# The start of a fused attention and expert kernel: x loaded first, a chain of norm steps split up and woven into the first tiles

## The chip, the cores and the metric

The kernel runs on one core of one Trainium2 chip, as one program. The metric is the device time of one execution in microseconds, the median of three runs. The core's engines are TensorE (PE), VectorE (DVE), ScalarE (ACT), GpSimd (POOL) and SyncE (SP), which here issues most transfers. Each engine works through its own queue in order; semaphores tie the queues together.

## The reference

x is [16, 256, 128] in fp32, 4096 tokens of 128 features. What is computed, cut to what matters here:

```python
x = x + layernorm(linear_attention(layernorm(x)))      # 16 heads of 8, q and k through elu + 1, causal
x = x + layernorm(ffn(layernorm(x)))                   # shared expert + 1 of 16 experts by a router

# linear attention, per batch and head, along the sequence:
s = s + outer(k_i, v_i);  z = z + k_i
out_i = (q_i @ s) / (q_i . z + 1e-6)                   # then @ Wo + bo
```

A layernorm here has no gain and no bias: (x - mean) / sqrt(var + 1e-5).

## The kernel before

The tokens are cut into 32 tiles of 128 (NT = 32), a tile to the 128 partitions, two tiles to a sequence. The kernel has three stages. Stage 1 (`step1`) walks over the 32 tiles and does norm, projection, causal sums and output projection. Stage 2 (`step2`) walks over 8 groups of four tiles and does the shared expert and the routing. Stage 3 (`step3`) walks over 47 tiles of rows sorted by expert. Nothing is planned at run time: each engine has its own copy of the loops, and the order written there is the order of its queue.

**Ahead of stage 1.** SyncE issues the attention weights `w_qkvo`, then x in three loads of 4, 12 and 16 tiles (LOADS), into the first 128 columns of the wide tile `rows` (260 columns a row: x, the attention's result, and four more), then the FFN's weights; then, once GpSimd has zeroed 15 tiles of `rows` (line 476, 3900 elements a partition), four transfers clear the table of sorted rows, and the expert weights follow. VectorE takes the statistics of each tile (line 708) and turns them into the reciprocal deviation `rs1` and the shift `nm1` by `rstd_steps` (lines 93 to 122), 15 small steps that depend on each other: the reciprocal root is a guess by bits and two rounds of Newton's method. It does so for two chunks (CHUNKS): tiles 0 to 3 at once, tiles 4 to 31 (128x28 elements a step) when all statistics are there. In between it writes constants and masks (lines 702 to 732), folds the mean into the projection weights (line 756, after TensorE's products of lines 1135 and 1137), makes the centring matrix (line 754) and, with ScalarE, splits the bias `bo` in three bf16 parts (line 743; `bias_row` on ScalarE, lines 550 and 553).

**A tile t of stage 1.** ScalarE norms x four tiles ahead (`xn`, line 567) and copies its transpose (`xnT`, 574). TensorE transposes (1105) and projects two tiles ahead (1117, q, k and v). ScalarE makes the parts of elu (589 to 594); GpSimd adds them (`qk`, 485) and makes the outer products (`kv`, 491, 128x1024, read from two tiles of SBUF). TensorE sums along the sequence with the triangular matrix `upto` (1086 for z, 1098 for kv, four instructions a tile, called here the tile's sum). VectorE does per tile, in this order: `zq` (777), for even tiles `carry` (782), for the tile before the reciprocal `rden` (786), `prod` (791), for the tile before `att` (801), then `den` (808), `num` (813), `rden` (818 or 822) and for odd tiles the carried part (827). `step1` on VectorE takes an iterator `others`, of which it issues `between` steps behind each of its own; from tile 28 on it is given the norm steps of stage 2 (`prepare_steps`).

TensorE projects tile t + 2 into the bank that VectorE's `zq` and `carry` of tile t must have read, and on even tiles it waits for the whole of tile t - 1 on VectorE before it goes on to transposes and projections.

## Time and profile before

| | |
|---|---|
| median of three runs | 337.07 us (335.73 to 337.62) |
| the profiled execution, its own time | 337.88 us |
| its span in the trace | 336.1 us |
| TensorE matmul busy | 272.1 us, 81% |
| VectorE busy | 278.6 us, 83% |
| ScalarE busy | 191.8 us, 57% |
| GpSimd busy | 189.7 us, 56% |
| mean granted TensorE clock | 0.92 |

The span is the time from the first to the last instruction that the profiler recorded; the execution's own time is 1.8 us more. A granted clock of 1.00 stands for the higher of TensorE's two levels (2.4 GHz) and 0.50 for the lower (1.2 GHz). The busy shares are means over the three stages; stage 1 takes roughly the first 140 us.

### The profile page before, as it was taken

Reading aid. Unit: us, or ns where it says so; the run is one execution under the profiler, and the core shown is the slowest. Engines: PE = TensorE matmul, PEld = TensorE weight load, DVE = VectorE, ACT = ScalarE, POOL = GpSimd, SP = SyncE. Lnnn points to the kernel's source line nnn. Section 1 sums busy time; section 2 is a strip of 40 time slices with the busy share of each in tenths; the row PEclk is TensorE's granted clock in tenths of the full one; section 3 lists DMA queues with packets and bytes.
Section 4 is the critical chain, followed back from the end, with each engine's and each line's share of the span. In section 5 each row is a group of like instructions: output and inputs, shape, how many; then the busy total and the mean of one; then the engine's idle time right before and its main releaser. Section 6 shows DMA issues by size and latency. Waiting matters only on the chain.

```text
span 336.1 us, 6349 instructions
## 1 busy us (share of the span) xinstructions
PE 272.1 (81%) x1535; PEld 191.2 (57%) x1535; DVE 278.6 (83%) x1109; ACT 191.8 (57%) x581; POOL 189.7 (56%) x215
## 2 busy tenths in 40 slices
PE   3459999999999994938888888988699999999100
PEld 1224555555655552515555555666599999999100
DVE  5998999999999999996599988971179999999800
ACT  2424565665656642357366666234699899997000
POOL 5064767777677773300035554764016788888770
PEclk9977999999999998765799999999799999999855
DMA  6999910000000000000001111221993101111100
GB/s 184 363 430 389 419 50 0 4 1 0 2 0 2 2 0 0 0 1 3 0 17 63 65 64 63 97 81 65 305 353 107 35 23 43 44 38 34 32 2 0
DMA packets 13701, 28.41 MB, mean 85 GB/s; under 512 B 1982, under 2 KB 10182, under 8 KB 12642
## 3 DMA queue, kind: packets, MB, share of 16 engines
q1 hardware_dynamic: 10480, 21.57, 17.8%
q0 software_dynamic: 3040, 6.37, 5.6%
q8 instruction: 14, 0.23, 0.3%
q14 instruction: 21, 0.17, 0.2%
q10 hardware_dynamic: 146, 0.07, 0.1%
HBM read 15.38 MB, written 13.60 MB: 86 GB/s over the span
## 4 chain that ended last, share of the span: by engine, by line
PE 41%; DVE 41%; issue 6%; DMA 3%; POOL 3%; ACT 2%; SPq 0%; ACTq 0%; POOLq 0%; DVEq 0%
PE banks L1098 14%; PE banks L1117 6%; DVE hT_e L1031 5%; PE banks L1193 4%; DVE rows L1038 3%; DVE hT L887 3%; DVE rows L1002 3%; PE banks L1126 2%; PE banks L1146 2%; POOL out L536 2%; PE banks L1148 2%; DVE stats L1053 2%; DVE stats L708 2%; PE banks L1086 2%; DMA rows<-in_x 2%
## 5 line engine op out<-in xcount | busy, mean ns | idle before, releaser
L1098 PE MATMUL banks<-kv,upto 128*128 128x512 f32 x128 | 64.3, 628 | 1.3 <-POOL kv L491 1.3
L491 POOL TENSOR_TENSOR kv<-qk,vv 128x1024 f32<-128x1024 f32 x32 | 62.4, 1950 | 2.5
L536 POOL DMA_INDIRECT out<-rows,token_i x47 | 46.8, 996 | 10.5 <-issue 6.2
L1246 PE MATMUL banks<-xsT,w_now 128*128 128x128 f32 x376 | 52.2, 283 | 0.4 <-DVE hT_e L1031 0.3
L485 POOL TENSOR_TENSOR qk<-ex,rl 128x256 f32<-128x256 f32 x32 | 23.3, 727 | 45.8 <-ACT ex L592 45.8
L1246 PEld LDWEIGHTS banks<-xsT,w_now 128*128 128x128 f32 x376 | 47.0, 196 | 1.3 <-issue 1.1
L518 POOL DMA_INDIRECT sorted_rows<-rows,slot_i x32 | 31.7, 990 | 25.5 <-DVE slot_i L877 17.5
L791 DVE TENSOR_TENSOR prod<-banks,qk 128x1024 f32<-128x1024 f32 x32 | 39.0, 1218 | 2.0 <-PE banks L1098 1.4
L813 DVE TENSOR_REDUCE num<-prod 128x128 f32<-128x1024 f32 x32 | 38.6, 1207 | 0.0
L1098 PEld LDWEIGHTS banks<-kv,upto 128*128 128x128 f32 x128 | 23.3, 201 | 18.3 <-issue 16.8
L1031 DVE TENSOR_TENSOR hT_e<-silu_e,banks 128x256 f32<-128x256 f32 x47 | 19.3, 410 | 16.3 <-ACT silu_e L690 13.9
L1117 PE MATMUL banks<-w_qkvo,xnT 128*128 128x384 f32 x64 | 28.4, 527 | 5.3 <-DVE carry L782 3.0
L1254 PE MATMUL banks<-w_exp_down,hT_e 128*128 x188 | 28.8, 276 | 0.9 <-DVE rows L1038 0.9
L528 POOL TENSOR_TENSOR rows<-rows 128x128 f32<-128x128 f32 x34 | 16.1, 475 | 22.5 <-DVE rows L1002 22.0
L694 ACT COPY w_now<-w_exp 128x512 f32 x47 | 28.7, 610 | 0.0
L574 ACT COPY xnT<-banks 128x128 f32<-128x128 f32 x32 | 8.5, 265 | 34.0 <-PE banks L1105 20.1
L1254 PEld LDWEIGHTS banks<-w_exp_down,hT_e 128*128 128x128 f32 x188 | 24.8, 192 | 1.3 <-issue 1.3
L682 ACT ACTIVATE xs<-rows 128x128 f32<-128x128 f32 x47 | 23.2, 493 | 3.1 <-SPq L460 2.8
L1193 PE MATMUL banks<-w_d,hT 128*128 128x128 f32 x128 | 16.4, 281 | 9.3 <-DVE hT L887 9.3
L567 ACT ACTIVATE xn<-rows,nm,rs 128x128 f32<-128x128 f32 x32 | 16.4, 517 | 10.2 <-DVE nm L122 10.2
L690 ACT ACTIVATE silu_e<-banks 128x256 f32<-128x256 f32 x47 | 18.1, 385 | 6.0 <-PE banks L1246 4.8
L1193 PEld LDWEIGHTS banks<-w_d,hT 128*128 128x128 f32 x128 | 14.9, 191 | 10.9 <-DVE hT L887 10.9
(179 smaller groups left out, 653.5 us busy)
## 6 DMA issues: line engine op xcount, KB each, us to landing
sorted_rows<-rows SPq DMA_DIRECT2D x3, 1950.0 KB, 13.3
rows<-sorted_rows SPq DMA_DIRECT2D x10, 520.0 KB, 6.4
w_exp<-in_gate_up SPq DMA_DIRECT2D x4, 1024.0 KB, 20.0
w_exp_out<-in_down SPq DMA_DIRECT2D x4, 512.0 KB, 20.1
rows<-in_x SPq DMA_DIRECT2D x1, 1024.0 KB, 11.1
rows<-in_x SPq DMA_DIRECT2D x1, 768.0 KB, 8.4
out<-rows,token_i POOLq DMA_INDIRECT x47
sorted_rows<-rows,slot_i POOLq DMA_INDIRECT x32
```

What stands on the lines that cost most here:

```text
L491: nc.gpsimd.tensor_tensor(kv[:, u, :].rearrange("p (h m d) -> p h m d", h=NH, m=HD), k, v, ALU.mult).then_inc(s_kv, 1)
L518: nc.gpsimd.indirect_dma_start(out=sorted_rows, out_offset=bass.IndirectOffsetOnAxis(ap=slot_i[:, t:t + 1], axis=0), in_=rows[:, t, :], in ...
L536: nc.gpsimd.indirect_dma_start(out=out_rows, out_offset=bass.IndirectOffsetOnAxis(ap=token_i[:, j - 1:j], axis=0), in_=rows[:, j - 1, 0:D] ...
L694: nc.scalar.copy(w_now[:, u % 2, :], flat(w_exp[:, bass.ds(e, 1), :])).then_inc(s_wn, 1)
L791: nc.vector.tensor_tensor(prod[:].rearrange("p (h m d) -> p h m d", h=NH, m=HD), ps_s[u % 2][:].rearrange("p (h m d) -> p h m d", h=NH, m=HD),
L813: nc.vector.tensor_reduce(num[:], prod[:].rearrange("p (n d) -> p n d", d=HD), AX, ALU.add).then_inc(s_chain, 1)
L1031: nc.vector.tensor_tensor(hT_e[:, u % 2, :], silu_e[:, u % 2, :], ps_gue[u % 2][:, F:2 * F], ALU.mult).then_inc(s_he, 1)
L1098: ins = nc.tensor.matmul(ps_s[u % 2][:, cols], upto[:], kv[:, u, cols], start=True, stop=True)
L1117: nc.tensor.matmul(ps_qkv[u % 2][:, 0:3 * D], xnT[:, u % 2, :], w_qkv, start=True, stop=True).then_inc(s_qkv, 1)
L1193: ins = nc.tensor.matmul(into, hT[:, f, k * P:(k + 1) * P], w_d[:, f, :], start=f == 0, stop=f == FC - 1)
L1246: ins = nc.tensor.matmul(ps_gue[u % 2][:, c * P:(c + 1) * P], w_now[:, u % 2, c * P:(c + 1) * P], xsT[:, u % 2, :], start=True, stop=True)
L1254: ins = nc.tensor.matmul(ps_ye[u % 2][:, 0:D], hT_e[:, u % 2, c * P:(c + 1) * P], flat(w_exp_down[:, bass.ds(e, 1), c, :]), start=c == 0, ...
```

## The change

- x has a tile of its own, `x_in`, contiguous over the tiles; the same memory is later the centred expert weights `w_exp_down`. Norm, statistics and the residual sum read x there. The loads are of 4, 4, 12 and 12 tiles, and the first stands ahead of the attention weights in SyncE's queue.
- GpSimd zeroes 6 tiles of `rows` instead of 15, and eight transfers clear the table instead of four.
- There are three chunks: tiles 0 to 3, 4 to 7 and 8 to 31. The first two use `norm_first`: five steps on VectorE, then a power of -0.5 on GpSimd (`tensor_tensor` with `ALU.pow`, 128x4, exponents in `minus_half`, written by ScalarE), then two steps on VectorE.
- The chain of the third chunk (`norm_rest`, the 15 steps, 128x24) is woven into VectorE's tiles 0, 1 and 2, one step behind each of the tile's own.
- On TensorE `stay_busy` issues small bf16 products whose result nobody reads: 8 ahead of the fold, 16 behind it, 16 at tile 0.
- The turning of the shared expert's weights (`w_down` by `centring`) goes behind the projection of tile 2 and into the bank `ps_o`; VectorE copies it (`w_d`) between tiles 0 and 1.
- On ScalarE the three bias parts go behind the elu parts of tiles 0, 1 and 2; more constants are written before x is waited for.

```diff
     CW = D + NH
...
         mean_row = sb("mean_row", [1, P])
...
         w_exp_out = sb("w_exp_out", [P, E, F])
-        w_exp_down = sb("w_exp_down", [P, E, FC, D])
+        x_then_down = sb("x_then_down", [P, E * FC, D])
+        x_in = x_then_down[:, 0:NT, :]
+        w_exp_down = x_then_down[:].rearrange("p (e c) d -> p e c d", c=FC)
...
-        CHUNKS = [(0, 4), (4, NT)]
-        LOADS = [(0, 4), (4, 16), (16, NT)]
+        CHUNKS = [(0, 4), (4, 8), (8, NT)]
+        LOADS = [(0, 4), (4, 8), (8, 20), (20, NT)]
+        CLEARED = 6
...
         s_mean = sem("mean_matrix_written")
...
         def _(sp):
-            sp.dma_start(w_qkvo[:], w_att).then_inc(s_w, 16)
             for c, (t0, t1) in enumerate(LOADS):
-                sp.dma_start(rows[:, t0:t1, 0:D], x_dram[:, t0:t1, :]).then_inc(s_x[c], 16)
+                sp.dma_start(x_in[:, t0:t1, :], x_dram[:, t0:t1, :]).then_inc(s_x[c], 16)
+                if c == 0:
+                    sp.dma_start(w_qkvo[:], w_att).then_inc(s_w, 16)
...
             sp.wait_ge(s_zero, 1)
...
             nc.gpsimd.memset(bias_rows[:], 0.0).then_inc(s_bias_clear, 1)
-            nc.gpsimd.memset(rows[:, NT:ST, :], 0.0).then_inc(s_zero, 1)
+            nc.gpsimd.memset(rows[:, NT:NT + CLEARED, :], 0.0).then_inc(s_zero, 1)
...
             nc.gpsimd.memset(rows[:, 0:NT, TOKEN + 1], 0.0)
+            pool.wait_ge(s_half, 1)
+            for c in range(2):
+                r = slice(*CHUNKS[c])
+                pool.wait_ge(s_variance1, c + 1)
+                nc.gpsimd.tensor_tensor(rs1[:, r], scratch1[:, 0, r], minus_half[:], ALU.pow).then_inc(s_rstd1, 1)
...
                 if g == 0:
...
-            act.wait_ge(s_bias, 16)
-            act.wait_ge(s_bias_clear, 1)
-            bias_row(0)
+            act.wait_ge(s_iota, 1)
+            nc.scalar.activation(minus_half[:], col_index[:, 0:GT], ACT.Copy, scale=0.0, bias=-0.5).then_inc(s_half, 1)
...
                     at_least(act, s_xn_t, t + 3)
-                    nc.scalar.activation(xn[:, u % 2, :], flat(rows[:, tiles(at), 0:D]), ACT.Identity,
+                    nc.scalar.activation(xn[:, u % 2, :], flat(x_in[:, tiles(at), :]), ACT.Identity,
...
                     nc.scalar.copy(xnT[:, (u + 3) % 2, :], ps_xT[:, 0:D]).then_inc(s_xnT, 1)
-                if t in (-2, 0):
-                    bias_row(1 if t else 2)
...
                     nc.scalar.copy(vv[:, u % 2, 0:D], ps_qkv[u % 2][:, 2 * D:3 * D]).then_inc(s_v, 1)
+                if t == -2:
+                    act.wait_ge(s_bias, 16)
+                    act.wait_ge(s_bias_clear, 1)
+                if t in (-2, -1, 0):
+                    bias_row(t + 2)
...
                 for t in range(t0, t1):
-                    yield nc.vector.bn_stats(stats[:, t, :], rows[:, t, 0:D])
+                    yield nc.vector.bn_stats(stats[:, t, :], x_in[:, t, :])
...
+            def norm_first(c, series):
+                r = slice(*CHUNKS[c])
+                mean_even, sq_even, mean_odd, sq_odd = (stats[:, r, n] for n in (1, 2, 4, 5))
+                ve, t, mean2 = (scratch1[:, n, r] for n in (0, 2, 3))
+                tensor, fused = nc.vector.tensor_tensor, nc.vector.scalar_tensor_tensor
+                series.wait()
+                yield series.done(tensor(t, mean_even, mean_odd, ALU.subtract))
+                yield series.done(fused(out=ve, in0=sq_even, scalar=D * EPS, in1=sq_odd, op0=ALU.add, op1=ALU.add))
+                series.wait()
+                yield series.done(fused(out=t, in0=t, scalar=0.25, in1=t, op0=ALU.mult, op1=ALU.mult))
+                yield series.done(tensor(mean2, mean_even, mean_odd, ALU.add))
+                series.wait()
+                yield fused(out=ve, in0=ve, scalar=1.0 / D, in1=t, op0=ALU.mult, op1=ALU.add).then_inc(s_variance1, 1)
+                dve.wait_ge(s_rstd1, c + 1)
+                yield series.done(tensor(t, mean2, rs1[:, r], ALU.mult))
+                series.wait()
+                yield nc.vector.tensor_scalar(nm1[:, r], t, -0.5, 1.0, ALU.mult, ALU.add).then_inc(s_norm1, 1)
...
             constants = constant_steps(Series(dve, s_mask_series, 0))
-            for _ in range(3):
+            for _ in range(6):
...
             dve.wait_ge(s_x[0], 16)
-            setup.done(finish(stats_of(*CHUNKS[0])))
-            for ins in norm_chunk(0, setup):
-                last = ins
-                next(constants, None)
-            last.then_inc(s_norm1, 1)
+            setup.done(finish(stats_of(*LOADS[0])))
+            for n, _ in enumerate(norm_first(0, setup)):
+                if n > 0:
+                    next(constants, None)
+                if n == 4:
+                    finish(constants)
+            dve.wait_ge(s_fold, 1)
+            nc.vector.tensor_tensor(w_qkv, w_qkv, ps_s[0][:, 0:3 * D], ALU.add).then_inc(s_folded, 1)
...
             nc.vector.tensor_tensor(centring[:], ident[:], neg_mean[:], ALU.add).then_inc(s_centring, 1)
-            dve.wait_ge(s_fold, 1)
-            nc.vector.tensor_tensor(w_qkv, w_qkv, ps_s[0][:, 0:3 * D], ALU.add).then_inc(s_folded, 1)
             dve.wait_ge(s_x[1], 16)
-            finish(stats_of(*LOADS[1]))
+            setup.done(finish(stats_of(*LOADS[1])))
+            chunk = norm_first(1, setup)
+            for _ in range(5):
+                next(chunk)
+            dve.wait_ge(s_x[2], 16)
+            for n, _ in enumerate(stats_of(*LOADS[2])):
+                if n >= 6:
+                    next(chunk, None)
             left_of_bias(0)
-            dve.wait_ge(s_x[2], 16)
-            setup.done(finish(stats_of(*LOADS[2])))
-            finish(norm_chunk(1, setup)).then_inc(s_norm1, 1)
+            dve.wait_ge(s_x[3], 16)
+            setup.done(finish(stats_of(*LOADS[3])))
...
-            dve.wait_ge(s_turned_d, 1)
-            nc.vector.tensor_copy(w_d[:].rearrange("p c d -> p (c d)"), ps_s[1][:, 0:FC * D]).then_inc(s_centred_d, 1)
-            def step1(t, u, others=iter(()), between=3):
+            def norm_rest():
+                for n, ins in enumerate(norm_chunk(2, setup)):
+                    if n == RSTD_STEPS + 1:
+                        ins.then_inc(s_norm1, 1)
+                    yield ins
+            def step1(t, u, others=iter(()), between=3, remaining=99):
...
                         other()
-                other(99)
+                other(remaining)
...
                         dve.wait_ge(s_ya, 2 * (s + 2) + 1 + half)
-                        xg = rows[:, tiles(GT * (s + 2) + 2 * half, 2), 0:D]
+                        two = tiles(GT * (s + 2) + 2 * half, 2)
                         yield nc.vector.tensor_tensor(
-                            xg, xg, ya[:, u % 2, 2 * half * D:2 * (half + 1) * D].rearrange("p (t d) -> p t d", d=D),
+                            rows[:, two, 0:D], x_in[:, two, :], ya[:, u % 2, 2 * half * D:2 * (half + 1) * D].rearrange("p (t d) -> p t d", d=D),
...
-            run_steps(dve, step1, 0, 4, 28, 28, 8, 4)
+            rest = norm_rest()
+            step1(0, 0, rest, 1, 0)
+            dve.wait_ge(s_turned_d, 1)
+            nc.vector.tensor_copy(w_d[:].rearrange("p c d -> p (c d)"), ps_o[:, 0:FC * D]).then_inc(s_centred_d, 1)
+            step1(1, 1, rest, 1, 0)
+            step1(2, 2, rest, 1)
+            run_steps(dve, step1, 3, 4, 28, 28, 8, 4)
...
+            def stay_busy(count):
+                for _ in range(count):
+                    nc.tensor.matmul(ps_o[:, 0:P], ones_bf[:], ones_bf[:], start=True, stop=True)
...
-                    pe.wait_ge(s_centring, 1)
-                    pe.wait_ge(s_w2, 16)
-                    for c in range(FC):
-                        ins = nc.tensor.matmul(ps_s[1][:, c * D:(c + 1) * D], w_down[:, c * P:(c + 1) * P], centring[:],
-                                               start=True, stop=True)
-                    ins.then_inc(s_turned_d, 1)
-                if t == 1:
+                    stay_busy(16)
+                if t == 2:
...
                                      start=True, stop=True).then_inc(s_qkv, 1)
+                if t == 0:
+                    pe.wait_ge(s_centring, 1)
+                    pe.wait_ge(s_w2, 16)
+                    for c in range(FC):
+                        ins = nc.tensor.matmul(ps_o[:, c * D:(c + 1) * D], w_down[:, c * P:(c + 1) * P], centring[:],
+                                               start=True, stop=True)
+                    ins.then_inc(s_turned_d, 1)
...
             nc.tensor.matmul(ps_s[0][:, 0:3 * D], mean_row[:], b_row[:], start=True, stop=False)
+            pe.wait_ge(s_const, 2)
+            stay_busy(8)
...
             nc.tensor.matmul(ps_s[0][:, 0:3 * D], neg_mean[:], w_qkv, start=False, stop=True).then_inc(s_fold, 1)
+            stay_busy(16)
...
```

## Rows read from the trace of the kernel before

**Rows 1.** Page, part 2: granted TensorE clock in 40 slices of 8.4 us.
```profile
PEclk9977999999999998765799999999799999999855
```
**Rows 2.** Windows: stretch, length, then busy us (instructions) of each engine; clock.
```profile
26.60:30.00 3.40, 3.40 (x6) 1.28 (x5) 2.28 (x6) 1.62 (x5) 2.14 (x2) 0.50 1.01 381
...
90.00:120.00 30.00, 29.94 (x136) 17.30 (x135) 29.79 (x69) 18.36 (x72) 22.75 (x17) 1.00 0.01 2
...
132.50:139.00 6.50, 5.09 (x13) 3.35 (x14) 5.80 (x17) 2.82 (x9) 2.32 (x2) 0.50 0.00 0
```
**Rows 3.** Timeline of VectorE, tiles 0 to 6: start, us, engine, line, operation.
```profile
25.04 0.28 DVE L777 TENSOR_TENSOR zq<-banks,qk 128x128 f32<-128x128 f32 x1
...
27.90 0.63 DVE L818 TENSOR_SCALAR rden<-den 128x16 f32<-128x16 f32 x1
...
30.24 1.23 DVE L791 TENSOR_TENSOR prod<-banks,qk 128x1024 f32<-128x1024 f32 x1 [1.35 <-PE banks L1098]
...
33.22 0.28 DVE L777 TENSOR_TENSOR zq<-banks,qk 128x128 f32<-128x128 f32 x1
...
47.36 0.28 DVE L777 TENSOR_TENSOR zq<-banks,qk 128x128 f32<-128x128 f32 x1
```
**Rows 4.** Chain of waits that ended last, its beginning: start us, us, what.
```profile
1.19 6.18 DMA rows<-in_x
7.39 0.88 DVE stats L708 x4
```
**Rows 5.** Timeline of all engines, 0 to 31 us.
```profile
1.84 3.34 POOL L476 MEMSET rows<- 128x3900 f32 x1
1.88 3.38 DVE L717 TENSOR_SCALAR upto<-col_index,row_index 128x128 f32<-128x128 f32 x1
...
3.75 1.65 PE L1137 MATMUL banks<-w_qkvo,neg_mean 128*128 128x384 f32 x2
...
11.32 0.17 DVE L122 TENSOR_SCALAR nm<-scratch 128x4 f32<-128x4 f32 x1
...
30.26 0.81 PE L1117 MATMUL banks<-w_qkvo,xnT 128*128 128x384 f32 x2
```
**Rows 6.** Timeline of all engines, the long chain: VectorE and GpSimd.
```profile
17.82 1.54 DVE L93 TENSOR_TENSOR scratch<-stats 128x28 f32<-128x28 f32 x1
...
20.06 1.95 POOL L491 TENSOR_TENSOR kv<-qk,vv 128x1024 f32<-128x1024 f32 x1
20.08 1.97 DVE L96 SCALAR_TENSOR_TENSOR scratch<-scratch 128x28 f32<-128x28 f32 x1
...
22.20 0.19 DVE L99 SCALAR_TENSOR_TENSOR scratch<-scratch 128x28 f32<-128x28 f32 x1
...
24.41 0.18 DVE L122 TENSOR_SCALAR nm<-scratch 128x28 f32<-128x28 f32 x1
```
**Rows 7.** DMA issues: what, queue, count, KB each, us from issue to landing.
```profile
w_qkvo<-in_w_att SPq DMA_DIRECT2D x1, 256.0 KB, 2.7
rows<-in_x SPq DMA_DIRECT2D x1, 256.0 KB, 6.2
```
**Rows 8.** Groups by line of GpSimd: busy us, mean ns of one, idle before.
```profile
L485 POOL TENSOR_TENSOR qk<-ex,rl 128x256 f32<-128x256 f32 x32 | 23.3, 727 | 45.8 <-ACT ex L592 45.8
...
L506 POOL TENSOR_TENSOR rows<-rstd,score 128x4 f32<-128x4 f32 x8 | 1.6, 204 | 0.7
```
**Rows 9.** Timeline, tiles 28 and 29, and the start of tile 30.
```profile
125.14 0.28 DVE L777 TENSOR_TENSOR zq<-banks,qk 128x128 f32<-128x128 f32 x1
...
129.13 1.95 POOL L491 TENSOR_TENSOR kv<-qk,vv 128x1024 f32<-128x1024 f32 x1
129.21 2.02 DVE L801 TENSOR_TENSOR att<-num,rden 128x128 f32<-128x128 f32 x1
...
133.48 0.28 DVE L777 TENSOR_TENSOR zq<-banks,qk 128x128 f32<-128x128 f32 x1
...
137.59 0.29 DVE L777 TENSOR_TENSOR zq<-banks,qk 128x128 f32<-128x128 f32 x1 [0.47 <-PE banks L1090]
```

12 lines of the change are left out of this document (8 added, 4 removed).

## The prediction

> **What bounds the kernel now.** I read the page first: TensorE's granted clock dips near the start, in the third and fourth of the 40 slices, and again before the middle [rows 1]. The windows then show the attention loop. From 90 to 120 us TensorE works 29.94 of 30 us and VectorE 29.79 [rows 2], and four tiles take 14.14 us (33.22 to 47.36), so 3.53 us a tile [rows 3]. That stretch is untouched by the change. What can move is when it starts, so I read the time before it step by step.
>
> The chain of waits begins with the first load of x, which lands at 7.39 us; VectorE works from then on without a pause [rows 4]. It does four statistics, the short deviation chain of chunk 0 (until 11.49), the fold, 28 more statistics, and then the long chain over 28 tiles, 17.82 to 24.59 us. Only at 25.04 does it touch tile 0 [rows 3, 5, 6]. The others are long ready: at 20.06 us GpSimd is already at the kv of tile 1 [rows 6]. So the start is bound by VectorE, and a microsecond saved there is one saved at the end, as long as the following tiles don't give it back.
>
> Two things inside the start matter. First, the long chain costs 6.8 us although its steps are 0.22 us apart when nothing disturbs them (ten intervals from 22.20 to 24.41): 15 steps are 3.3 us, the other 3.5 us are steps that ended only when a GpSimd instruction ended. The step of line 96 took 1.97 us, beside an instruction of GpSimd from 20.06 to 22.01 [rows 6]. Statistics, reductions and the product from PSUM don't stretch so: the product at 30.24 took its usual 1.23 us beside GpSimd's kv. Second, VectorE waits 1.35 us ahead of the product at 30.24, for TensorE, which ran at the lower of its two clocks from 26.6 to 30 us [rows 2, 3].
>
> **The change, part by part.** The sum is made up to the start of tile 2 (its first VectorE instruction, at 33.22 us in this execution [rows 3]), since behind it both kernels run the same queues.
>
> *x first, its own tile, smaller zero block.* The first transfer of the program, 256 KB in the same layout as x's first load has in its new tile, took 2.7 us from its issue at 0.74 us; x's first load, second in line and in pieces of a row each, took 6.2 [rows 7]. So x should be there at about 3.5 us. VectorE isn't free then: `upto` ended at 5.26 with GpSimd's zeroing of 3900 elements, 3.34 us [rows 5]. With 1560 elements that is 1.34 us, ending at 3.2; four small constants behind it bring VectorE to about 4.0. Statistics start at 4.0 instead of 7.39: 3.4 us gained. The later x loads are wanted at 7, 9 and 12 us and lie ahead of everything large; I cost them at nothing. If one were late, VectorE would stand in order behind it. The eight clearing transfers in place of four carry the same bytes, wait on SyncE's queue ahead of expert weights that nobody needs before the routing ends, and cost nothing.
>
> *The projection weights, now second.* The fold on TensorE (1.65 us in this trace [rows 5]) must be over when VectorE has finished chunk 0, at about 7.3 us, so the weights must land by 5.6. With x's 256 KB ahead and no small pieces I expect 4.5. Taken as late as the old second transfer (7.39), they would cost 1.7 us.
>
> *Chunk 0 with a GpSimd power.* Today it lasts from 8.27 to 11.49 us, 3.2 us [rows 4, 5]. New: five steps with three mask operations between them, 1.3 us; two hand-overs of about 0.1; the power; two steps, 0.4. The trace has no power. The nearest from below is GpSimd's multiply over 128x4, 0.20 us [rows 8]; from above I take the dearest tensor operation it has, 1.95 us [rows 6]; nothing excludes a dearer one. A power is more than a multiply, over just four elements: I take 0.6. That makes 2.4 us, 0.8 gained.
> The Trainium skill (GPSIMD Engine Reference, 3.1 Elementwise) gives some 2.6 cycles an element for a two-input operation, and 12 for branching on data; by that the power would cost hardly more than the multiply, an estimate of 0.25 us, and the sum would be 0.35 us better. No row here has a power, so nothing bears it out yet.
>
> *Chunk 1 (tiles 4 to 7), new on VectorE.* Five steps and two, 1.4 us lost; its power lies behind six statistics (0.2 us each [rows 4]), so it is free up to 1.2 us.
>
> *Bias parts moved on ScalarE.* Tile 0's halves no longer wait behind a bias part. The two differences on VectorE now meet GpSimd's work on tiles 0 and 1; 0.2 us lost.
>
> So far 3.4 + 0.8 - 1.4 - 0.2 = 2.6. Without its long chain VectorE would reach tile 0 today at 25.04 - 6.8 = 18.2; new 15.6 us. ScalarE and GpSimd keep up: chunk 0 is ready 3.4 + 0.8 = 4.2 us earlier, and the chain behind it no longer holds the bias part, so kv(1), which started at 20.06, starts near 15.5, just ahead of VectorE's first woven step.
>
> *The long chain in tiles 0 to 2.* One step behind each VectorE instruction: six in tile 0, eight in tile 1, the last in tile 2. Today tiles 0 and 1 take 8.18 us (25.04 to 33.22), in which are the wait of 1.35 and a stall of 0.46 (line 818 took 0.63 instead of 0.17) [rows 3]: 6.4 us of work. New: 6.4 + 14 x 0.22 = 9.5, plus the stalls. GpSimd has five instructions in that time (kv of tiles 1, 2, 3 and qk of 2, 3): at worst VectorE waits out all, 3 x 1.95 + 2 x 0.73 = 7.3 us; at best none. The nearest row is tile 28, where the norm steps of the next stage are woven in already: it lasts 8.34 us (125.14 to 133.48) instead of 3.53, and its att at 129.21 took 2.02 us, beside a kv that began at 129.13 [rows 9], against 0.28 us for zq, an operation of the same size [rows 3]. That is 1.7 us of stall in one tile, so 3.5 for two. Here the very first step meets kv(1) as well, which is 1.5 to 1.9 more: I take 5.0. Tiles 0 and 1 then last 14.5 us, and tile 2 starts at 15.6 + 14.5 = 30.1 instead of 33.22: 3.1 us gained.
>
> *TensorE kept busy.* 8, 16 and 16 small bf16 products; TensorE has idle time in front of each that is longer than they are, save that the 16 behind the fold may hold the first transpose by 0.4 us, which the statistics of x hide. What they buy lies before the weave and VectorE doesn't wait for it. But TensorE has some 3.5 us of work in tile 1, and VectorE now needs 7 us for it, so TensorE stands idle for about 4. At tile 28 the same happened: the clock was at its lower level from 132.5 to 139 [rows 2], and tile 29 took 4.11 us instead of 3.53 [rows 9]. So the clock falls again just when tile 2 starts: with a part of the following tile, 0.8 us lost. Bounds: nothing, and 1.9, if one more tile loses what tile 1 loses today (1.35 [rows 3]) beside the 0.58 of tile 29.
> The Trainium skill (TensorE: Matmul & The Clock Gate, Part 1) says that the lower level is the resting state and activity lifts it. The granted clock's column reads 1.00 in the first windows, before any change was recorded, yet the fold's two products took 1.65 us, where the projection's two of the same width took 0.81 at 30.26 [rows 5]; this sides with the page. By the page alone the small products would keep the clock up from the start and the 0.8 would not be lost: the sum would be 3.1. It names no cure for a wait as long as that of tile 1.
>
> Net: 3.1 - 0.8 = 2.3 us. The span of 336.1 becomes 333.8, the execution's own 337.88 becomes 335.6. The median, 337.07, lies 0.8 below the profiled one; against it the forecast is **334.8 us**.
>
> **Rivals.**
> *The weave slips between.* Stalls of 0 to 2.5 us instead of 5.0, no clock loss: a gain of 4.8 to 8.1, about **331**. For it: each GpSimd instruction can hold one step only, and the 1.2 us instructions of VectorE cover half of a kv. Against it: in tile 28 they covered too little.
> *The weave swallows it.* Stalls 7.3 and a clock loss of 1.9, or the weights at 7.39: the gain shrinks to somewhere between -1.1 and 1, about **336.7**: no change.
> *The power is dear (other side).* Chunk 0's power stands on VectorE's path in full, chunk 1's beyond 1.2 us. At 4 us each they cost 3.4 + 2.8 = 6.2 more than reckoned: **341**. It decides from about 2.7 us: 2.1 + 1.5 = 3.6 eats the gain and goes 1.3 beyond. For it: no row has a power; against it: it is four elements.
> *It doesn't do what it says.* The products leave the clock as it was: nothing changes in the sum, since it counts nothing for them.
>
> **How the numbers follow.** Forecast case, gain 1 to 4.5 us: 0.47, of which some 0.05 falls short of 1.7 us. The weave slips between: 0.17. Swallowed: 0.24. Power dear: 0.08; something else that is late: 0.04. A measurement here tells about 0.5%, 1.7 us, from no change. Faster: 0.42 + 0.17, and a little of the swallowed case, 0.60; slower 0.08 + 0.04 + 0.01 = 0.13; the same 0.27. The range goes from the middle of the good case, 331.0, to 338.2, the swallowed case's bad end (337.07 + 1.1); the forecast case alone is 332.5 to 336.
>
> **What the profile after would show.** First statistics at about 4 us (late: x or the constants). The power under 1 us and the second step behind it within 0.2. The fold done by 7 us. Tile 0 begun at 15 to 16 us. In tiles 0 and 1 woven steps of 0.5 to 2 us, each ending with a GpSimd instruction, 5 us in sum; tile 2 begun at about 30; the granted clock at its lower level around 30 to 33; then 7.06 us a pair as before. I would be wrong above all through the stalls, the power, and the landing of the weights.

## The result, and the profile after

The changed kernel takes 334.98 us (median of 20 runs, 330.13 to 336.4), the kernel before in the same sessions 338.27 us (335.73 to 340.32). The ratio 0.9858 [0.9827, 0.989], like every ratio below, leaves out runs that lie over 1.5% above the fastest run of their kernel, which here takes away ten of the changed kernel's 20, the profiled one among them, and none of the kernel before; the medians over all runs give 0.990. The profiled execution of the changed kernel took 335.17 us, its span is 333.4 us (before 337.88 and 336.1), its mean granted clock 0.92 in both.

The page's clock row dips in the fourth slice, 25 to 33 us, and not again until the sixteenth; that of before dips in the third and fourth [rows 1]:

```profile
PEclk9996999999999998785899999999799999999655
```

VectorE's timeline from the first statistics to the start of tile 4 (start, duration, engine and line, operation, tiles, shapes, count, and the idle time before it with what ended it):

```profile
3.90 0.87 DVE L723 BATCH_NORM_STATS2 stats<-x_then_down 128x6 f32<-128x128 f32 x4 [0.34 <-DMA x_then_down<-in_x]
...
7.17 0.16 DVE L745 TENSOR_TENSOR scratch<-scratch,rs 128x4 f32<-128x4 f32 x1 [1.13 <-POOL rs L491]
...
8.41 0.56 DVE L788 TENSOR_TENSOR w_qkvo<-w_qkvo,banks 128x384 f32<-128x384 f32 x1 [0.88 <-PE banks L1196]
...
16.34 0.28 DVE L821 TENSOR_TENSOR zq<-banks,qk 128x128 f32<-128x128 f32 x1
16.54 1.81 DVE L93 TENSOR_TENSOR scratch<-stats 128x24 f32<-128x24 f32 x1
...
21.89 0.28 DVE L821 TENSOR_TENSOR zq<-banks,qk 128x128 f32<-128x128 f32 x1
22.09 1.41 DVE L104 TENSOR_TENSOR scratch<-scratch 128x24 f32<-128x24 f32 x1
...
25.17 1.92 DVE L110 SCALAR_TENSOR_TENSOR scratch<-scratch 128x24 f32<-128x24 f32 x1
...
27.21 0.17 DVE L113 TENSOR_TENSOR scratch<-scratch 128x24 f32<-128x24 f32 x1
27.30 1.21 DVE L857 TENSOR_REDUCE num<-prod 128x128 f32<-128x1024 f32 x1
...
29.02 0.28 DVE L821 TENSOR_TENSOR zq<-banks,qk 128x128 f32<-128x128 f32 x1
...
35.27 1.23 DVE L835 TENSOR_TENSOR prod<-banks,qk 128x1024 f32<-128x1024 f32 x1 [2.35 <-PE banks L1147]
...
38.26 0.28 DVE L821 TENSOR_TENSOR zq<-banks,qk 128x128 f32<-128x128 f32 x1
```

The same stretch on GpSimd:

```profile
1.84 1.39 POOL L484 MEMSET rows<- 128x1560 f32 x1
...
6.09 1.04 POOL L491 TENSOR_TENSOR rs<-scratch,minus_half 128x4 f32<-128x4 f32 x1 [2.56 <-DVE scratch L743]
...
16.35 1.95 POOL L504 TENSOR_TENSOR kv<-qk,vv 128x1024 f32<-128x1024 f32 x1
...
25.08 1.97 POOL L504 TENSOR_TENSOR kv<-qk,vv 128x1024 f32<-128x1024 f32 x1
```

And on TensorE:

```profile
6.73 1.65 PE L1196 MATMUL banks<-w_qkvo,neg_mean 128*128 128x384 f32 x2 [2.01 <-DMA w_qkvo<-in_w_att]
...
10.88 0.87 PE L1166 MATMUL banks<-w_qkvo,xnT 128*128 128x384 f32 x2
...
29.07 0.48 PE L1154 MATMUL banks<-ident,xn 128*128 128x128 f32 x1 [3.43 <-DVE num L871]
...
32.23 3.01 PE L1147 MATMUL banks<-kv,upto 128*128 128x512 f32 x4
```

**How far ahead each tile is.** A tile starts with its `zq`. Before, tiles 0, 2 and 4 start at 25.04, 33.22 and 40.30 us [rows 3] (the last is in the same timeline). Now they start at 16.34, 29.02 and 38.26: a lead of 8.70, then 4.20, then 2.04, and 1.80 at tile 16. So 4.5 us go between tiles 0 and 2, where the long chain now lies, and 2.4 more by tile 5. The first loss is the place of the chain, which cost 6.8 us ahead of tile 0 before. The copy of `w_d`, 0.33 us, has moved the same way, from just ahead of tile 0 to just behind it. The second loss is a real one. TensorE stands idle for 3.43 us ahead of its instruction at 29.07, waiting for VectorE to finish tile 1; then tile 3's sum at 32.23 takes 3.01 us, and VectorE waits 2.35 us for it at 35.27.

### The profile page after: what moved, and what is told of

Read it like the earlier page. It is cut to its first block, busy times and chain, and to the rows that moved or that the text cites. A ratio compares the mean times of both kernels' runs of the same rounds, so it can differ in the third digit from the quotient of the medians.

```text
span 333.4 us, 6437 instructions
## 1 busy us (share of the span) xinstructions
PE 273.1 (82%) x1575; PEld 194.2 (58%) x1575; DVE 276.1 (83%) x1108; ACT 191.5 (57%) x582; POOL 190.5 (57%) x217
## 4 chain that ended last, share of the span: by engine, by line
DVE 42%; PE 41%; issue 6%; DMA 3%; POOL 3%; ACT 2%; SPq 0%; DVEq 0%; POOLq 0%; ACTq 0%
PE banks L1147 13%; PE banks L1166 5%; DVE hT_e L1081 5%; PE banks L1253 4%; DVE rows L1088 3%; PE banks L1183 3%; DVE hT L931 3%; DVE rows L1052 3%; PE banks L1206 2%; POOL out L549 2%; PE banks L1208 2%; DVE stats L1103 2%; PE banks L1306 2%; PE banks L1135 2%; DMA w_qkvo<-in_w_att 2%
## 5 line engine op out<-in xcount | busy, mean ns | idle before, releaser
L1147 PE MATMUL banks<-kv,upto 128*128 128x512 f32 x128 | 62.1, 608 | 1.3 <-POOL kv L504 1.3
L1314 PE MATMUL banks<-x_then_down,hT_e 128*128 x188 | 28.8, 276 | 0.6 <-DVE rows L1088 0.6
L1314 PEld LDWEIGHTS banks<-x_then_down,hT_e 128*128 128x128 f32 x188 | 24.8, 192 | 1.0 <-issue 1.0
L1206 PE MATMUL banks<-xmT,w_ffn 128*128 128x512 f32 x32 | 19.5, 693 | 0.8 <-ACT xmT L624 0.8
## 6 DMA issues: line engine op xcount, KB each, us to landing
w_exp<-in_gate_up SPq DMA_DIRECT2D x4, 1024.0 KB, 20.8
```

Of the source, the lines that this page charges most:

```text
L1147: ins = nc.tensor.matmul(ps_s[u % 2][:, cols], upto[:], kv[:, u, cols], start=True, stop=True)
L1314: ins = nc.tensor.matmul(ps_ye[u % 2][:, 0:D], hT_e[:, u % 2, c * P:(c + 1) * P], flat(w_exp_down[:, bass.ds(e, 1), c, :]), start=c == 0, ...
```

## The experiments

Three sets of four ran, each set on one chip with the kernel before beside it (the column "before" is its median there). A lead is the start of a tile on VectorE in the kernel before minus that in the experiment, from one trace each (before: 25.04, 33.22, 43.73 for tiles 0, 2, 5). The column "lead stage 3" is the same for TensorE's first product of stage 3, at 238.78 us before.

| kernel | set | tile 0 at | lead tile 2 | lead tile 5 | lead stage 3 | us | before | ratio |
|---|---|---|---|---|---|---|---|---|
| changed | | 16.34 | 4.20 | 1.79 | 2.73 | 334.98 | 338.27 | 0.9858 [0.9827, 0.989] |
| changed_again | 1 | 17.59 | 4.57 | 2.81 | 0.63 | 338.12 | 341.47 | 0.9884 [0.9819, 0.9949] |
| filled_wait | 1 | 15.91 | 4.61 | 4.53 | 4.93 | 334.35 | 341.47 | 0.9799 [0.9752, 0.9847] |
| no_small_products | 1 | 18.67 | 3.49 | 2.17 | 1.65 | 336.89 | 341.47 | 0.9877 [0.9822, 0.9933] |
| chain_in_one_block | 1 | 20.71 | 4.21 | 4.21 | 4.28 | 337.1 | 341.47 | 0.9873 [0.983, 0.9916] |
| power_undone | 2 | 18.37 | 3.78 | 2.02 | −1.21 | 339.26 | 341.56 | 0.9941 [0.9907, 0.9974] |
| filled_and_weights_by_scalar | 2 | 16.70 | 3.82 | 3.74 | 4.27 | 336.09 | 341.56 | 0.9853 [0.9808, 0.9899] |
| x_first_alone | 2 | 22.52 | 1.58 | 1.41 | −0.84 | 338.17 | 341.56 | 0.9903 [0.9869, 0.9936] |
| third_power | 2 | 16.71 | 7.71 | 4.52 | −0.52 | 337.91 | 341.56 | 0.9829 [0.975, 0.9907] |
| four_powers | 3 | 20.13 | 3.26 | 0.19 | 1.50 | 337.57 | 338.25 | 0.9976 [0.9952, 1.0001] |
| two_chunks | 3 | 20.82 | 3.88 | 3.88 | 6.94 | 330.94 | 338.25 | 0.9783 [0.9743, 0.9824] |
| filled_wait_again | 3 | 16.06 | 4.47 | 4.39 | 6.11 | 331.95 | 338.25 | 0.9808 [0.9768, 0.9849] |
| changed_third | 3 | 16.63 | 3.90 | 1.14 | 2.27 | 334.59 | 338.25 | 0.9878 [0.9833, 0.9922] |

### The changed kernel again, twice

No edit; they give the changed kernel on the chips of sets 1 and 3.

> The changed kernel, unchanged, beside the next three. In its first profile the lead over the kernel before was 8.7 us at the start of tile 0, 6.6 at tile 1, 4.2 at tile 2, 2.0 at tile 4 and 1.8 from there on. Both theories: the same leads within 0.5 us if the clock falls at the same place, and a time 1 to 1.5% below the kernel before.

> The changed kernel, unchanged, a third time. Its lead at tile 5 was 1.8 us in one profile and 2.8 in the other, by when the clock came back (after 6.8 or 3.4 us at the lower level). Expected: one of the two leads, and a time 1 to 1.4% below the kernel before.

VectorE's timeline of *changed_again*:

```profile
8.41 0.54 DVE L788 TENSOR_TENSOR w_qkvo<-w_qkvo,banks 128x384 f32<-128x384 f32 x1
...
13.46 1.45 DVE L777 TENSOR_TENSOR bias_left<-bias,bias_part 128x128 f32<-128x128 f32 x1
...
17.59 0.28 DVE L821 TENSOR_TENSOR zq<-banks,qk 128x128 f32<-128x128 f32 x1
17.79 0.18 DVE L93 TENSOR_TENSOR scratch<-stats 128x24 f32<-128x24 f32 x1
```

The ratio repeats: 0.9884 and 0.9878. The trace of *changed_again* differs in two instructive points. x landed a microsecond later (first statistics at 4.86 instead of 3.90), and yet VectorE added the fold at 8.41 us in both traces: the wait for the weights swallowed the delay. Tile 0 began 1.25 us later all the same, because GpSimd was at tile 0 earlier (kv(0) at 12.81 instead of 13.63) and its work held chunk 1's last step and the first bias difference, 0.53 and 1.45 us instead of 0.15 and 0.57. Then tile 2 began 0.37 us earlier, at 28.65: the first woven step took 0.18 us, since it came when kv(1) was over, against 1.81 in the first trace. A delay of tile 0 was swallowed by a stall that it avoided.

### The idle time in tile 1 filled: filled_wait

```diff
             def step1(t, u):
...
+                if t == 2:
+                    stay_busy(56)
                 if not odd and live(t - 1, NT):
                     pe.wait_ge(s_chain, CH * t)
```

> 56 small products behind TensorE's sum of tile 2, in the 3.4 us in which it waits for tile 1 on VectorE. Theory (the fall of the clock takes back 2.2 us): the clock stays at its higher level through tiles 2 and 3, tile 4 starts near 36.1 us instead of 38.3, the lead at tile 5 is about 4.0 us, and the time falls by about 2.2 us against the changed kernel. Rival (VectorE would have lost the time anyway, since its lead is used up by the end of the weave): the clock stays up, yet tile 5 starts within 0.5 us of 41.9. A second rival: the products overshoot and delay the transposes of tile 2; then the lead at tile 4 is under 2.

> The kernel with the filled wait a second time, beside the changed kernel on the same chip. If 1.7 to 2.7 us less in the first pair of runs was the clock and not the chip: 0.4 to 1% less than the changed kernel again, lead at tile 5 about 4.5 us; if it was chance, the two are within 0.3%.

TensorE's timeline of *filled_wait*, and the same window of the changed kernel, of this one and of the next experiment (columns: window, its length, busy time of PE, PEld, DVE, ACT and POOL, granted clock, DMA share, GB/s):

```profile
25.05 3.29 PE L1123 MATMUL banks<-ones_bf 128*128 128x128 bf16 x56
...
30.61 1.88 PE L1149 MATMUL banks<-kv,upto 128*128 128x512 f32 x4
```

The changed kernel:

```profile
27.50:34.40 6.90, 5.33 (x12) 3.02 (x13) 5.39 (x17) 2.16 (x8) 1.88 (x2) 0.51 1.02 412
```

*filled_wait*:

```profile
27.50:34.40 6.90, 6.33 (x42) 3.97 (x39) 6.78 (x21) 3.61 (x15) 2.69 (x2) 1.00 1.01 412
```

*chain_in_one_block*:

```profile
27.50:34.40 6.90, 6.88 (x31) 3.77 (x30) 6.79 (x16) 4.19 (x18) 5.35 (x4) 1.00 1.02 415
```

With 56 small products in the wait the granted clock is 1.00 through the window where it was 0.51, and tile 3's sum takes 1.88 us instead of 3.01. The lead of tile 2 is what it was (4.61 against 4.57 on the same chip); that of tile 5 is 4.53 against 2.81. So the theory held: the loss behind tile 2 is the clock's, shown by taking its cause away with nothing else changed. It repeats in set 3: 4.39 against 1.14. In time: 0.9799 and 0.9808 against 0.9884 and 0.9878; the two intervals of each pair still overlap a little, but the difference came twice and in the expected size. The rule of the Trainium skill (TensorE: Matmul & The Clock Gate, Part 1), that activity lifts the clock out of a lower resting state, agrees with these rows.

### The weave taken out: chain_in_one_block

```diff
-            rest = norm_rest()
+            finish(norm_rest())
+            rest = iter(())
             step1(0, 0, rest, 1, 0)
```

> The chain of the third chunk (15 steps, 128x24) in one block ahead of tile 0 instead of woven in; all else as changed. Theory: a step that waits for the one before costs 0.22 us in the block and 0.1 us between other instructions, and in both places GpSimd holds some of them back by 3 to 5 us in all. So the block costs 3.3 + 3 to 4 us ahead of tile 0 (tile 0 at 23 to 23.7 us), tiles 0 and 1 then take 6.4 to 7 us, and tile 2 starts at 29.5 to 30.7 instead of 29.0: 0.5 to 1.7 us later. Rival (the weave costs more than it brings, through its stalls and the long idle time of TensorE in tile 1): tile 2 starts earlier than 29.0, the clock doesn't fall at tile 2, and tile 5 starts before 41.9.

VectorE's timeline of this run:

```profile
16.03 0.19 DVE L93 TENSOR_TENSOR scratch<-stats 128x24 f32<-128x24 f32 x1
16.14 1.95 DVE L94 SCALAR_TENSOR_TENSOR scratch<-stats 128x24 f32<-128x24 f32 x1
...
20.71 0.28 DVE L821 TENSOR_TENSOR zq<-banks,qk 128x128 f32<-128x128 f32 x1
...
26.02 1.23 DVE L835 TENSOR_TENSOR prod<-banks,qk 128x1024 f32<-128x1024 f32 x1 [1.28 <-PE banks L1148]
...
29.01 0.29 DVE L821 TENSOR_TENSOR zq<-banks,qk 128x128 f32<-128x128 f32 x1
```

GpSimd's, which says why only one step is long:

```profile
16.04 2.00 POOL L504 TENSOR_TENSOR kv<-qk,vv 128x1024 f32<-128x1024 f32 x1
24.05 0.73 POOL L498 TENSOR_TENSOR qk<-ex,rl 128x256 f32<-128x256 f32 x1 [6.01 <-ACT ex L602]
```

Tile 2 starts at 29.01 us; woven it started at 29.02 and 29.32, and on this chip, in *changed_again*, at 28.65. The theory, by which it would start at 29.5 or later without the weave, fell; the weave, the largest part of the change, brings at most 0.4 us at tile 2, and at tile 5 the block is ahead by 1.4 us (39.52 against 40.92 on this chip). In one block the chain meets kv(1) alone and then has GpSimd idle for 6.01 us: one stall of 1.95 us, 4.7 us in all where it was 6.8 before. Woven, the steps are hidden better but three of them meet kv's. And in one block TensorE stands idle for 3.93 us already ahead of its projection at 21.36; its lower clock comes early, at 20.7 to 24.1 us, and not again in these tiles. VectorE pays for it with the wait of 1.28 us in tile 1, and the lead of 4.21 stands unchanged at tile 5. The ratio, 0.9873, can't be told from that of the changed kernel on the same chip, although the lead at stage 3 is 3.65 us larger in the two traces.

### The small products left out: no_small_products

The three calls of `stay_busy` are deleted, and with the first of them TensorE's wait for the constant that it multiplies.

> All 40 small products left out (8 and 16 around the fold, 16 at tile 0). My prediction costed them at nothing. Theory: the projections of tiles 0 and 1 run at the lower clock (1.5 us a pair of instructions instead of 0.87), GpSimd starts its first product 1 to 1.5 us later, but VectorE starts tile 0 within 0.7 us of 16.34, because it has its own statistics to do; the sum of tile 0, at 3.4 us instead of 2.0, ends after the first woven step, so tile 2 starts at most 1 us later. Rival (they pay): tile 0 or tile 2 starts over 1 us later and the time rises by 1 us or more.

```profile
9.00 0.56 DVE L788 TENSOR_TENSOR w_qkvo<-w_qkvo,banks 128x384 f32<-128x384 f32 x1 [1.44 <-PE banks L1192]
...
12.56 0.67 DVE L745 TENSOR_TENSOR scratch<-scratch,rs 128x4 f32<-128x4 f32 x1
...
13.36 1.91 DVE L747 TENSOR_SCALAR nm<-scratch 128x4 f32<-128x4 f32 x1
```

And TensorE's:

```profile
7.32 1.65 PE L1192 MATMUL banks<-w_qkvo,neg_mean 128*128 128x384 f32 x2 [3.38 <-DMA w_qkvo<-in_w_att]
```

In VectorE's timeline above, the wait for the fold grows to 1.44 us from 0.88. That isn't the products' doing: the fold takes TensorE 1.65 us with them and without, and it began at 7.32 because the weights landed later in this execution, 6.1 us from their issue where the three traces of the changed kernel have 5.5, 4.9 and 5.4. Chunk 1's two last steps, which ran for 0.14 and 0.15 us behind statistics in the first trace, now meet GpSimd's work and take 0.67 and 1.91. Tile 0 begins at 18.67, 1.1 us later than in *changed_again* and 2.3 later than in the first trace; the lead at tile 2 is 3.49 against 3.90 to 4.57, and at tile 5 it is 2.17, inside the changed kernel's 1.14 to 2.81.

What the products do is seen on TensorE. Its projections of 128x384 for the first two tiles take 1.55 and 1.37 us without them (1.55 and 1.49 in the kernel before) and 0.87 and 0.81 with them: they do lift the clock. VectorE waits for none of these. So the rival's microsecond at tile 0 is there, but one trace can't tell the products from the late weights, and the time doesn't show it: 0.9877 against 0.9884.

### Power on VectorE again: power_undone

Chunks 0 and 1 take the 15 steps of `norm_chunk` instead of `norm_first`; GpSimd's two powers are gone, and chunk 1's steps are spread over the statistics.

> Chunks 0 and 1 by VectorE's 15 steps as chunk 0 was before, no power on GpSimd; all else as changed. In the changed kernel VectorE waits 1.13 us for the power of chunk 0 (GpSimd took 1.04 us for it), and then for the fold. Theory (the power brings almost nothing here, since the fold is what VectorE waits for behind it): chunk 0 ends 0.5 to 0.9 us later (ten more steps of 0.2 us, less the 1.3 of power and hand-overs), the wait for the fold goes, and chunk 1 costs 8 more steps between statistics, at 0.1 us each. Tile 0 starts 0.5 to 1.5 us later than 16.34. Rival (it saves the eight steps it replaces, twice): tile 0 starts 2.5 us or more later and the time rises by 1% of the span.

Tile 0 begins at 18.37, 0.8 to 2.0 us later than in the three traces of the changed kernel; the lead at tile 2 is 3.78, 0.1 to 0.8 less than theirs, and at tile 5 2.02, among theirs. The theory had the mechanism for chunk 0: it ends at 7.95 us, 0.4 later than in the first trace, and the wait for the fold is gone, so that VectorE is at chunk 1's statistics 0.6 us earlier. What is lost lies in chunk 1: three of its steps now meet GpSimd's work and take 0.51, 1.90 and 0.57 us instead of 0.15, 2.5 us in all. By tile 2 most of it is gone: the result lies between theory and rival. The ratio, 0.9941 [0.9907, 0.9974], lies above those of the changed kernel, from other chips though.

### The weights on ScalarE's queue: filled_and_weights_by_scalar

*filled_wait*, and the load of `w_qkvo` issued by ScalarE ahead of the bias instead of by SyncE behind x's first load.

> The kernel with the filled wait, and the attention weights issued as the first transfer of ScalarE's queue instead of the second of SyncE's. Theory (the weights, landing at 6.7 us, hold the fold and VectorE by 0.5 to 0.9 us): they are issued 0.4 us earlier and share the transfer engines with x's first load, land at 5 to 6 us, the fold is done before chunk 0, VectorE doesn't wait for it, and the lead at tile 5 rises from 4.5 to about 5. Rival: both loads then land later than the first did, at 4.5 us or more, and what the fold gains is lost on the statistics: lead at tile 5 between 4.0 and 4.6.

```profile
4.95 1.61 PE L1195 MATMUL banks<-b_row,mean_row 1*128 1x384 f32 x2 [4.95 <-DMA b_row<-in_b_qkv]
```

The lead at tile 5 is 3.74, against 4.53 and 4.39 with SyncE's queue: the theory fell, and the rival's 4.0 was too high as well. But the edit did more than it was meant to do. The projection's bias `b_row` stands behind the weights in ScalarE's queue now; TensorE's product with it, in the row above, began at 4.95 us instead of 2.12, and so the fold began at 7.32, a microsecond later than in *filled_wait* (6.30), though the weights had landed 4.3 us from an issue at 0.72. VectorE's wait for the fold fell to 0.46 us only because VectorE came later itself: x landed late, first statistics at 4.85. That may be the company of the weights, but in *changed_again* x came at 4.86 without any such edit. So whether x loses what the weights win isn't shown; that this placement doesn't pay is.

### x first and nothing else: x_first_alone

On the kernel before: the tile of its own for x, x's first load ahead of the weights, and 6 tiles zeroed; loads, chunks and chain as they were.

> The kernel before, with x in a tile of its own, loaded ahead of the attention weights (loads of 4, 12 and 16 tiles as before), and the smaller zero block; no power, no third chunk, no small products, nothing woven in. Theory (the early x is the main part of the gain): the first statistics start at 3.8 to 5.3 instead of 7.39 us (behind `upto`, which now ends at 3.3, come the masks in chunk 0 as before), tile 0 starts 2.2 to 3.4 us earlier than 25.04 and keeps it: lead at tile 5 of 2 to 3.5 us, time 0.6 to 1% less than before. Rival (the fold, late since the weights come second, and another meeting of chain and GpSimd eat it): lead at tile 5 under 1.5 us.

```profile
15.29 1.55 DVE L93 TENSOR_TENSOR scratch<-stats 128x28 f32<-128x28 f32 x1
16.76 0.76 DVE L94 SCALAR_TENSOR_TENSOR scratch<-stats 128x28 f32<-128x28 f32 x1
17.55 1.97 DVE L96 SCALAR_TENSOR_TENSOR scratch<-scratch 128x28 f32<-128x28 f32 x1
...
28.66 1.22 DVE L795 TENSOR_TENSOR prod<-banks,qk 128x1024 f32<-128x1024 f32 x1 [2.76 <-PE banks L1102]
```

VectorE's timeline: 3.2 us gained at the first statistics (4.23 against 7.39), 2.52 at tile 0, and 1.58 at tile 2. The long chain takes 6.8 us as before, with three long steps; it moved together with the kv's that it meets. Then tile 1's product waits 2.76 us instead of 1.35 [rows 3], for a sum that TensorE made in 3.62 us, where it takes 1.88 at the higher clock. So half of a gain at the head was given back two tiles later, and the lead of 1.41 at tile 5 is the rival's case; the ratio of 0.9903 is what the theory had.

### A third power, and a fourth

*third_power*: the chunk of 24 tiles is done by `norm_first` too, its five steps in tile 0, its power on GpSimd behind kv(3), its last two steps in tile 3. *four_powers*: chunks of 4, 4, 12 and 12 tiles, all by `norm_first`; the third's steps among the statistics, its power behind kv(1).

> The reciprocal deviations of the third chunk by a power on GpSimd too (128x24), behind its tile 3; VectorE has five steps woven into tile 0 and two into tile 3. It measures the power: 1.04 us for 128x4. If each element costs the same on top of a fixed 0.2 us, 24 take about 5.2 us; if the instruction is mostly a fixed cost, under 2. Theory (5.2 us): VectorE's tile 1 is 3 to 4 us shorter than 7.1, tile 2 starts near 25.5, but GpSimd has the power ahead of kv of tile 4 and delays that: the lead at tile 5 is between 2 and 5 us. Rival (under 2 us): nothing is delayed, and the lead at tile 5 is over 5 us.

```profile
25.51 0.28 DVE L825 TENSOR_TENSOR zq<-banks,qk 128x128 f32<-128x128 f32 x1
...
31.51 0.70 DVE L749 TENSOR_TENSOR scratch<-scratch,rs 128x24 f32<-128x24 f32 x1 [2.47 <-POOL rs L509]
```

GpSimd, the same run:

```profile
27.24 4.23 POOL L509 TENSOR_TENSOR rs<-scratch,minus_half 128x24 f32<-128x24 f32 x1
```

Tile 2 begins at 25.51 us, a lead of 7.71: tile 1 without woven steps takes 3.37 us instead of 7.13. But the power of 24 values takes 4.23 us of GpSimd (the theory had 5.2), VectorE waits 2.47 us for it, and at tile 5 the lead is 4.52, as with the wait filled: the theory was right on both tiles.

> Four chunks (tiles 0 to 3, 4 to 7, 8 to 19, 20 to 31), all with the power on GpSimd. The power took 1.04 us for 4 elements and 4.1 for 24, so about 0.4 + 0.155 an element: 2.3 us for 12. The first five steps of the third chunk go between statistics, its power between GpSimd's tiles 1 and 2 (2.4 us of idle time in the changed kernel), its last two steps into tile 1; the fourth chunk's steps go into tiles 2 and 8, its power behind GpSimd's tile 5. Theory (the 14 steps woven into tiles 0 and 1 and their 4.7 us of stall are what tiles 0 and 1 still lose): tile 2 starts at 25 to 26.5 us instead of 29.0, TensorE is never idle for 2 us in tile 1, so the clock doesn't fall; the fourth chunk's power costs 1 to 1.5 us in tile 6; lead at tile 10 of 5 to 6.5 us. Rival (each power holds VectorE's steps as kv does, and GpSimd is the bound of these tiles): lead at tile 10 under 4.5 us.

```profile
13.60 1.79 DVE L745 TENSOR_TENSOR scratch<-stats 128x12 f32<-128x12 f32 x1
...
16.20 1.89 DVE L748 SCALAR_TENSOR_TENSOR scratch<-scratch 128x12 f32<-128x12 f32 x1
...
26.98 1.23 DVE L850 TENSOR_TENSOR prod<-banks,qk 128x1024 f32<-128x1024 f32 x1 [2.55 <-PE banks L1164]
...
30.16 1.51 DVE L745 TENSOR_TENSOR scratch<-stats 128x12 f32<-128x12 f32 x1
```

This one came out worse than the theory, and by another mechanism than the rival's. The variance steps of the third chunk fell beside kv(0) and kv(1) (1.79 and 1.89 us in VectorE's timeline); tile 0 began at 20.13; TensorE stood idle for 3.27 us and was at its lower clock from 19.8 to 26.7, and tile 1's product waited 2.55 us. In tile 2 the steps of the fourth chunk met a kv (1.51 us at 30.16) and stretched the tile, so that the next kv met another instruction (1.86 us at 34.93): tile 2 lasted 6.7 us, and the lead went from 3.26 to −0.19. It is −2.4 from tile 10 on, behind the fourth power (2.28 us on GpSimd). The ratio is 0.9976 [0.9952, 1.0001].

The rival held that a power holds VectorE as a kv does. It doesn't, as a line of GpSimd's timeline and one of VectorE's show:

```profile
41.80 2.28 POOL L492 TENSOR_TENSOR rs<-scratch,minus_half 128x12 f32<-128x12 f32 x1
41.95 0.28 DVE L860 TENSOR_TENSOR att<-num,rden 128x128 f32<-128x128 f32 x1
```

`att` took its usual 0.28 us in the midst of the power; the next one, at 45.09, took 1.85 beside a kv that began at 44.85.

### The simplest version: two_chunks

```diff
-        CHUNKS = [(0, 4), (4, 8), (8, NT)]
+        CHUNKS = [(0, 4), (4, NT)]
...
-            rest = norm_rest()
+            finish(norm_rest())
+            rest = iter(())
```

The code of the chunk of tiles 4 to 7 goes with it, its power too. What is left is x first, chunk 0 with the power, and everything else in one chain ahead of tile 0; the small products stay.

> Only two chunks (tiles 0 to 3 with the power, 4 to 31 by the long chain in one block), all else as in the kernel with the chain in one block, whose lead was 4.2 us at tile 2 and at tile 5. It tells what the small second chunk brings. Theory (it costs VectorE 1.4 us and brings it nothing at once, but lets ScalarE norm tile 4, and TensorE transpose and project, before the long chain is over): tile 0 starts up to 1.4 us earlier than 20.7, but tile 2 no earlier than 29.0, since its xn, transpose and projections come after the chain. Rival (the small chunk is a pure cost): the lead at tiles 2 and 5 is 5 us or more.

```profile
16.19 1.96 DVE L94 SCALAR_TENSOR_TENSOR scratch<-stats 128x28 f32<-128x28 f32 x1
...
20.82 0.28 DVE L819 TENSOR_TENSOR zq<-banks,qk 128x128 f32<-128x128 f32 x1
...
29.34 0.28 DVE L819 TENSOR_TENSOR zq<-banks,qk 128x128 f32<-128x128 f32 x1
```

VectorE's timeline shows one stalled step and tile 2 at 29.34 us, 0.33 later than with three chunks, and the lead of 3.88 us holds to tile 5. Neither expectation was met in full: tile 0 began no earlier than with three chunks (20.82 against 20.71), among other things because VectorE now waited 0.88 us for x's third load, and the rival's lead of 5 us didn't come. At 330.94 us it is the fastest that ran: 0.9783 [0.9743, 0.9824], against 0.9878 [0.9833, 0.9922] for the changed kernel on the same chip. The intervals of *two_chunks* and *filled_wait_again* overlap; both lie wholly below the kernel before, and only that of *two_chunks* lies wholly below the changed kernel's as well.

## Why the prediction was right, and where it was not

The forecast was 334.8 us with the sign "faster", and the median is 334.98. The direction and the course of it (a large lead at tile 0, half of it lost in the weave, more to the clock) were right. The agreement to 0.2 us is luck in two ways. Terms that were off cancel: the weave took 1.8 us less than forecast, while tile 0 began 0.7 us later and the clock cost 1.6 more. And the forecast is a gain of 2.3 us taken from a median of 337.07, while the kernel before has a median of 338.27 over its 20 runs: the gain was 3.3 us.

**Start of the statistics: right.** 3.90 us against 4.0.

**Weights, costed at nothing: wrong.** Forecast to be there at 4.5 us, they took 5.5 us from an issue at 1.17; the fold began at 6.73, and VectorE waited 0.88 us for it. The bound of 1.7 held.

**Chunk 0: 2.8 us against 2.4.** The power takes 1.04 us, not 0.6, and VectorE waits 1.13 for it. It is inside the bounds, far from the 2.7 at which that rival decides. The figure worked out from the Trainium skill (GPSIMD Engine Reference, 3.1 Elementwise), 0.25 us, was four times too low; the measurement decides.

**Chunk 1: about 0.7 us against 1.4.** Its five steps lie between 9.98 and 10.61 us; its last two stretched twelve statistics from 2.4 to 2.5 us. **Bias:** the two differences took 0.57 and 0.46 us instead of 0.27 each, 0.5 lost against 0.2. With all of this tile 0 began at 16.34 against 15.6.

**The weave: 12.7 us for tiles 0 and 1 against 14.5.** The stalls were right: lines 93, 104, 108 and 110 ran 4.7 us over, against 5.0. The mis-sized term is "14 x 0.22". Steps of the long chain stand 0.22 us apart because each waits for the one before: in chunk 1's five steps of this trace, those that need the one before start 0.20 and 0.19 us behind it, the others 0.08. Between independent instructions the wait is hidden, and a woven step costs about 0.1 (line 113 fills 27.21 to 27.30). Left out of the sum was the copy of `w_d`, 0.33 us, which now lies between tiles 0 and 1: (12.7 − 4.7 − 6.4 − 0.3) / 14 = 0.09. Tile 2 began 1.1 us earlier than forecast.

**The clock: 2.4 us lost against 0.8.** The mechanism was the one named, TensorE idle in tile 1; *filled_wait* shows it. The size failed: the estimate took a part of one following tile from tile 28, while here the lower clock held from 27.7 to 34.5 us, over the transposes and the projection at 29.07 to 31.4 and all of tile 3's sum. The size isn't fixed either: TensorE's idle time ahead of tile 2's transpose was 3.43 or 3.44 us in all three traces of the changed kernel, and the lower clock held for 6.8, 3.4 and 6.8 us; the lead fell by 2.4, 1.8 and 2.8. The bound of 1.9 was too low for two of the three.

**The small products, costed at nothing: nothing here contradicts it.** They lift the clock for the first projections, and VectorE waits for none of what that speeds up. Without them tile 2 began 0.4 to 1.1 us later, but the weights had also landed later in that trace; at tile 5 and in the time no difference is left.

**"A microsecond saved there is one saved at the end, as long as the following tiles don't give it back": the condition failed, and the traces say where.** Eight traces of five kernels have this weave (the changed kernel, *filled_wait*, *no_small_products*, *power_undone*, *filled_and_weights_by_scalar*). They fall into two groups. Where tile 0 begins at 15.91 to 16.70 us, tile 2 begins 12.68 to 12.70 later; where it begins at 17.59 to 18.67, tile 2 begins 11.06 or 11.07 later. The difference is the first woven step: 1.81 us beside kv(1) in the first group, 0.18 or 0.19 in the second, where kv(1) is over. Within a group a microsecond at tile 0 is a microsecond at tile 2, to a few hundredths; between the groups 1.6 us are given back at once. So tile 2 begins at 28.6 to 29.7 us in all eight, and it does too in the two kernels that have the chain in one block, with tile 0 at 20.7 and 20.8.

**The rivals.** "The weave slips between" is written for a gain of 4.8 to 8.1 without a clock loss; with stalls of 2.5 instead of 5.0 and no clock loss the sum gives 5.6 at its lower end, 4.8 only with the 0.8 taken off. It had the right time for a version with the clock kept up (331.95 in *filled_wait_again*), not by the mechanism that it named. "Swallowed" came nearest in the size of its clock loss (1.9 against 2.4), not in its stalls. The power was not dear at four values; at twelve and 24 it was (2.28 and 4.23 us). "It doesn't do what it says" was wrong: the small products lift the clock of the first projections (0.87 and 0.81 us against 1.55 and 1.49 before), which is worth nothing to VectorE, as the sum had it.

**Left open, and where it lies.** The time and the lead at tile 5 don't go together well. By the medians over all runs the changed kernel is faster by 3.3, 3.4 and 3.7 us on three chips, at leads of 1.8, 2.8 and 1.1 us, and *four_powers* by 0.7 us although it is 2.4 us behind from tile 10 on. The traces show where the rest is. From TensorE's first product of stage 3 to the end all fourteen take 96.9 to 97.8 us. But from the start of tile 31 on VectorE to that product they take anything from 89.1 to 97.9 us, and this goes with the mean granted clock in the same stretch: 89.1 us at 0.94 (*four_powers*), 90.5 at 0.93 (*two_chunks*), 93.1 at 0.91 (the kernel before), 96.0 at 0.89 (*changed_again*), 97.9 at 0.87 (*third_power*). The changed kernel alone has 92.1, 92.0 and 96.0. So one execution differs from the next by up to 4 us in stage 2, more than the change brings. A lead at stage 3, from one trace each, therefore says little, and the per cent between *chain_in_one_block* and *two_chunks*, alike in their leads, lies in this stretch (93.3 and 90.5 us) and can't be put down to the second chunk. Why the clock stays low longer in one execution than in another, and whether the change itself moves the odds of it, no run here isolates.

## What to carry to other kernels

Before weaving a chain of small steps into a loop, try it in one block at a time when the engine that stalls it is idle; the block cost one stall here where the weave cost three, and it stretched no tile. Where a stretched tile can't be avoided, look at TensorE's idle time in it and fill it: 56 products nobody reads were worth more than the weave. And judge an earlier start by a tile behind the disturbance, not by the first, and from more than one trace: which instructions meet differs from one execution to the next.
